# Gated 3x3 convolution pair on one core: four PSUM banks for each sum, the base group 6 units behind, residuals last in a round

## The reference

```python
def qconv_cg(x, w, theta):
    base = cin // CG_GROUPS                       # 64 // 4 = 16 channels
    yp = conv3x3(x[:, :base], w[:, :base])
    yr = conv3x3(x[:, base:], w[:, base:])
    d = jax.nn.sigmoid(CG_ALPHA * (yp - theta[None, :, None, None]))
    return yp + d * yr
...
h = jax.nn.relu(bn(qconv_cg(x, w_a, theta_a), gamma_a, beta_a, mean_a, var_a))
h = bn(qconv_cg(h, w_b, theta_b), gamma_b, beta_b, mean_b, var_b)
return jax.nn.relu(x + h)
```

## Time and profile before

| | |
|---|---|
| median of 3 runs | 456.45 us (455.68 to 456.56) |
| profiled execution, its own time | 456.05 us |
| span from first to last instruction in it | 454.2 us |
| PE busy | 439.9 us (97%) |
| DVE busy | 246.3 us (54%) |
| ACT busy | 209.0 us (46%) |
| matmuls of L383 | 7776, in 1944 units of each of four groups |
| read and written in HBM | 13.14 MB and 12.85 MB |

### The profile page before, as it was taken

One profiled execution on the slowest core, in us unless ns is written; L12 is line 12 of the kernel. 1 busy time (PEld: TensorE's weight loads), 2 busy tenths in 40 slices (PEclk: granted clock), 3 DMA queues, 4 the chain that ended last, 5 costly groups with the idle time before them and its releaser, 6 DMA issues.

```text
span 454.2 us, 16832 instructions
## 1 busy us (share of the span) xinstructions
PE 439.9 (97%) x7801; PEld 436.1 (96%) x7801; DVE 246.3 (54%) x405; ACT 209.0 (46%) x334; POOL 6.8 (1%) x22
## 2 busy tenths in 40 slices
PE   4999999999999999999999999999999999999992
PEld 4999999999999999999999999999999999999992
DVE  6445565365456537544653754575365546435534
ACT  5455645454454445435444533544365344425313
POOL 5000000000000000000000000000000000000000
PEclk9999999999999999999999999999999999999996
DMA  9930000080806280070626044052622121003126
GB/s 164 215 76 2 4 3 1 3 144 2 144 1 113 35 143 4 4 142 3 116 29 144 2 84 63 1 104 43 115 33 47 29 54 21 3 1 74 25 50 141
DMA packets 116388, 27.05 MB, mean 60 GB/s; under 512 B 116192, under 2 KB 116192, under 8 KB 116320
## 3 DMA queue, kind: packets, MB, share of 16 engines
q1 hardware_dynamic: 115408, 25.86, 31.9%
q10 hardware_dynamic: 592, 0.13, 0.1%
q0 software_dynamic: 320, 0.00, 0.0%
HBM read 13.14 MB, written 12.85 MB: 57 GB/s over the span
## 4 chain that ended last, share of the span: by engine, by line
PE 96%; DMA 2%; DVE 1%; ACT 1%; issue 0%; DVEq 0%
PE acc L383 95%; DMA out_dram<-rows_out 1%; DMA w_nat<-in_L_conv_w_a_dram 1%; PE acc L339 1%; DVE rows_out L630 0%; DVE mix L615 0%; DVE mix L613 0%; ACT w_pad L450 0%; ACT rows_out L507 0%; ACT w_hi L443 0%; DVEq L612 0%
## 5 line engine op out<-in xcount | busy, mean ns | idle before, releaser
L383 PE MATMUL acc<-h_hi,w_hi 32*128 32x512 f32 (+1 forms) x1248 | 270.0, 389 | 0.0
L383 PE MATMUL acc<-h_lo,w_hi 32*128 32x512 f32 (+1 forms) x1248 | 268.9, 389 | 0.0
L383 PE MATMUL acc<-x_hi,w_hi 32*128 32x456 f32 x1344 | 267.8, 371 | 0.8 <-ACT w_hi L443 0.8
L383 PE MATMUL acc<-h_hi,w_lo 32*128 32x512 f32 (+1 forms) x1248 | 268.1, 388 | 0.0
L383 PE MATMUL acc<-x_hi,w_lo 32*128 32x456 f32 x1344 | 267.0, 369 | 0.0
L383 PE MATMUL acc<-x_lo,w_hi 32*128 32x456 f32 x1344 | 266.6, 368 | 0.0
L383 PEld LDWEIGHTS acc<-x_hi,w_hi 32*128 32x128 f32 x1344 | 218.9, 187 | 2.3 <-issue 0.9
L383 PEld LDWEIGHTS acc<-x_lo,w_hi 32*128 32x128 f32 x1344 | 218.8, 185 | 0.4
L383 PEld LDWEIGHTS acc<-x_hi,w_lo 32*128 32x128 f32 x1344 | 218.8, 186 | 0.3
L383 PEld LDWEIGHTS acc<-h_hi,w_lo 32*128 32x128 f32 x1248 | 201.1, 183 | 0.2
L383 PEld LDWEIGHTS acc<-h_lo,w_hi 32*128 32x128 f32 x1248 | 200.9, 183 | 0.2
(11 more groups left out here) (52 smaller groups left out, 30.3 us busy)
## 6 DMA issues: line engine op xcount, KB each, us to landing
x<-in_x_dram SPq DMA_DIRECT2D x30, 392.0 KB, 5.2
out_dram<-rows_out SPq DMA_DIRECT2D x30, 392.0 KB, 7.3
out_dram<-rows_out SPq DMA_DIRECT2D x4, 126.0 KB, 2.5
x<-in_x_dram SPq DMA_DIRECT2D x1, 280.0 KB, 4.9
x<-in_x_dram SPq DMA_DIRECT2D x1, 266.0 KB, 5.7
w_nat<-in_L_conv_w_a_dram SPq DMA_DIRECT2D x1, 144.0 KB, 3.1
w_nat<-in_L_conv_w_b_dram SPq DMA_DIRECT2D x1, 144.0 KB, 4.3
x<-in_x_dram ACTq DMA_DIRECT2D x1, 126.0 KB, 3.2
```

Of the source, the lines that this page charges most:

```text
L383: return pe.matmul(sums(bank, blk), w[g * ROWS:(g + 1) * ROWS, tap], moving(blk, part, c, dx, g), start=(u == 0 and (alone or g == FIRST_G ...
```

## The change

yr and yp get four banks each (`b % 4` and `4 + b % 4`). The base group runs 6 units behind group 1, as group 2 does, in place of 20. The transposes of the second weights and of the parameter rows, both in place of steps 13 and 16, are issued at step 5, and the parameter rows go to bank 4. On ACT all four gates of a round come first, each with its x split, then all four finishes. On DVE two x splits, then four products with their sums, then the other two splits, then the four residuals or low parts.

```diff
-YR_BANKS, YP_BANKS = 5, 3
+YR_BANKS, YP_BANKS = 4, 4
-OFFSET = (20, 0, 6, 12)
+OFFSET = (6, 0, 6, 12)
...
-                if step == 13:
+                if step == 5:
                     pe.wait_ge(wlo_ready, 2)
                     weights(1, 6)
-                if step == 16:
+                if step == 5:
                     pe.wait_ge(prmdup_ready, 2)
-                    pe.transpose(psum[:, 5, 0:10], prm_dup[:].rearrange("n c q -> n (c q)"),
+                    pe.transpose(psum[:, 4, 0:10], prm_dup[:].rearrange("n c q -> n (c q)"),
...
-                    if g == 0 and u == 0 and b == 1:
+                    if g == 0 and u == 0 and b == 2:
                         pe.wait_ge(whi_ready, 4)
                         pe.wait_ge(wlo_ready, 4)
...
             for b in range(0, TOTAL, ROUND):
+                for j in range(ROUND):
+                    gate(b + j)
+                    split_ahead(b + j)
+                for j in range(ROUND):
+                    finish(b + j)
...
                 nc.vector.tensor_tensor(mix_rows(b), mix_rows(b), yp_rows(b), ALU.add).then_inc(mixed_ready, 1)
-                if order[b][0] == "b":
-                    residual(b)
...
             for b in range(0, TOTAL, ROUND):
+                for j in range(2):
+                    split_ahead(b + j)
+                for j in range(ROUND):
+                    mix_sums(b + j)
+                for j in range(2, ROUND):
+                    split_ahead(b + j)
+                for j in range(ROUND):
+                    if order[b + j][0] == "b":
+                        residual(b + j)
+                    else:
+                        low_parts(b + j)
```

More of the change, by code:

```diff
@@ L568, in batch_norms @@
                 dve.wait_ge(prmT_ready, 1)
-                nc.vector.tensor_copy(prm[:].rearrange("p k n -> p (k n)"), psum[:, 5, 0:10]
+                nc.vector.tensor_copy(prm[:].rearrange("p k n -> p (k n)"), psum[:, 4, 0:10]
                                       ).then_inc(rvar_ready, 1)
```

## The result

The changed kernel takes 461.33 us in the median of 4 runs (461.18 to 461.62), against 456.45 us (455.68 to 456.56) before. The ratio is 1.0116, with a 95% interval from 1.0101 to 1.0130: slower by 1.2%, where 1.4% was forecast (462.6 us, range 460.2 to 465.3). The profiled execution took 461.62 us with a span of 459.8 us, 5.6 us more than the span before. "The kernel before" and "the changed kernel" are always these two; an experiment's time is given beside the kernel before in the same session, which differed from session to session by up to 0.8 us.

What follows compares the result with a forecast made beforehand. The prediction took PE to bound the 26 rounds, with costs only at the two ends: span 454.2 + 2.3 (start) + 0 (rounds) + 4.2 (end) = 460.7 us, plus 1.85 around it, 462.6 us; range 460.2 to 465.3.

Steps and rivals of the forecast that it cites:

- What bounds the kernel: Whole kernel: a start, 26 rounds bound by PE, and an end of some 14 us; the change moves the ends.
- The start: Before the first product: all groups stand behind the base group's wait for the parameter copy; 2.3 us slower, bounds 1.9 and 3.4.
- 3.2 us behind the fourth group: At the start: PE's clock rises 3.2 us after the fourth group enters at 17.4, so at 20.6 us.
- The rounds: The 26 rounds: four banks still give products enough time; cost 0, bounds -1.4 and +1.5 us.
- The spare 0.35 to 0.4 us at the yr banks: In the rounds: with four banks each product ends 0.35 to 0.4 us before PE needs it, less some 0.1.
- The end: Last round: place 104's residual stands behind four products and sums, so SP's stores start 4.2 us later without shrinking; bounds 3.3, 4.2.
- three pairs of 1.43 us and one of 1.31: Last round on DVE: four products with sums before the first residual, from 440.38 to 445.98 us.
- The sum: Whole kernel: span 454.2 + 2.3 + 0 + 4.2 = 460.7 us, plus 1.85 around it: 462.6 us.
- Rival 1: Rounds: the spare 0.4 us isn't enough; 467.6 us with 0.2 us lost in 25 rounds, 483 in lockstep; chance 0.10.
- the 483 given for the rival's worst case: Rounds: groups in lockstep in all rounds, 0.8 us lost a round, 483 us.
- Rival 2: End: the stores close up behind the last relu, which then sets the end; 457.2 us; chance 0.06.
- Rival 3: Rounds: every one of 26 rounds lost 0.3 us to three yp banks; 7.8 us given back, 454.8; chance 0.02.

Runs made afterwards that it cites:

- e2: The changed kernel with the old order in the last round (each residual right behind its sum, ACT's first relu behind two gates): 457.43 us, ratio 1.0037 to the kernel before.
- e5: The changed kernel with each residual right behind its sum again on DVE, in all rounds: 484.38 us beside 455.86 us of the kernel before.
- e9: The changed kernel with image 14 stored in two parts, its first 23 slots at once: 459.10 us, ratio 1.0074 to the kernel before.
- e4: The kernel before with only its last round in the changed order: 461.67 us, ratio 1.0136 to the kernel before.
- e1: The changed kernel with the parameter rows transposed into bank 3 in place of bank 4: 457.69 us, ratio 1.0044 to the kernel before.
- e8: The kernel before with both transposes at step 5 in place of steps 13 and 16: 454.98 us, ratio 0.9987 to the kernel before.
- e3: The changed kernel with parameter rows in bank 3 and the old order in the last round: 453.85 us, ratio 0.9958 to the kernel before.
- e6: The changed kernel with the base group 12 units behind in place of 6: 475.88 us (2 runs).
- e7: The kernel of e3, with ACT issuing one of the two stores of each piece of the last image: 454.65 us, ratio 0.9973 to the kernel before.
- e10: The changed kernel with parameter rows in bank 3, old order in the last round and image 14 stored in two parts: 452.69 us, ratio 0.9934 to the kernel before.

## Why the prediction was right, point by point

**What bounds the kernel** held: PE's rounds are the same 412 us in both kernels, and all that moved moved at the ends.

**The start**: forecast +2.3 us, measured +2.3 (30.38 against 28.07), by the steps given. The copy ended at 15.23 (15.42 forecast), behind the low and high parts of the weights and image 1's split, just as the chain lists them. The clock reached its upper level at 20.7 (20.6 forecast from "3.2 us behind the fourth group"). That agreement is luck. In kernels with this same start the units came to 0.21 us apart at 19.4 (e2), 20.7 (after), 21.2 (e5) and 21.5 us (e9), which is 2.3 to 4.1 us behind the fourth group's first unit; with the start of before it was 3.2 us in one execution and 1.7 us in the other (e4). The runs give no fixed distance. The first product of kernels with this same start came at 29.67 (e2), 30.38 (after), 30.63 (e5) and 30.72 us (e9), and those with the start of before at 27.33 (e4) and 28.07: means of 30.35 and 27.70, 2.65 us apart, with 0.7 to 1.1 us between executions of one start. What the wait costs beside a kernel without it is more, 3.3 us (e1), since moving the transposes up gains some 0.6 us (e8) once nothing else holds the start.

**The rounds**: forecast 0 between -1.4 and +1.5, measured -0.4 us. It repeats: 412.2 to 412.4 us in the kernels with the old order (before, e4, e8), 411.8 to 411.9 in those with the new one (after, e1, e2, e3). Which part of the change gives the 0.4 us was not tested. The spare 0.35 to 0.4 us at the yr banks was enough, and e5, which takes 0.7 to 1.4 us from it, lost what this reading said, 25.6 us for 26. How many steps PE's sequencer runs ahead of its waits was not tested by itself.

**The end**: the mechanism held, the size was 0.5 us smaller. The term that failed is "three pairs of 1.43 us and one of 1.31": I took the distance from product to next product out of the kernel before, where each operation waits for the result of the one ahead of it. In the changed kernel the product of the next block does not depend on the sum ahead of it, and starts 0.60 us behind it (442.96 to 443.56) in place of 0.71; so does the first residual (446.81 to 447.35). Product to residual took 5.10 us in place of 5.60. From there on 0.77 us to the relu, 0.74 to the store and 8.77 us of stores were as read.

**The sum**: 460.7 us of span forecast, 459.8 measured: 0.5 us of the end, 0.4 us of the rounds. Its own time lies 1.8 us above the span, as added, and 0.3 us above the median of its runs. As a difference to the kernel before, 6.5 us were forecast; the two profiled executions differ by 5.6 us, and the ratio gives 5.3. The range was not added from the bounds as given: it takes 4.4 us for the end where the text had at most 4.2, and -1.0 for the rounds where it had -1.4. With the bounds as given it is 459.9 to 465.2 us, and the measured time lies in either.

**The rivals.** Rival 1 (the spare time isn't enough) did not happen, but e5 and e6 show that it was near: one edit takes the kernel to 484 us. That this is near the 483 given for the rival's worst case is chance, since e5 delays the products by 0.7 to 1.4 us, which the changed kernel does not do. Rival 2 (stores close up) is excluded by SP's 8.76 or 8.77 us in seven profiles (before, after, e1 to e5), and by e7. The Trainium skill's fit ("DMA: Bandwidth & Descriptors", anatomy of a DMA) is given there for one DMA on the GpSimd path; applied to SP's ten stores together, as the prediction did, it gives an estimated 5.7 us from the first store to the last byte's landing. The traces do not agree: from SP's first issue to the end of the span it is 10.9 us in both kernels, 8.8 of them in the issues, at 157 to 173 GB/s (e3, e7) in packets of under 512 B. Rival 3 (the rounds hold more waiting) had 0.4 us to give, not 7.8.

## What to carry to other kernels

When PE is busy 97% of the time, read the two ends: which transfer is the last one, what is queued behind it, and which instruction first lets it start. An order that is good for the steady rounds (products first) can be bad for the last round, where nothing needs the bank any more and the first result is what starts the stores; give the last round its own order, and store early what is complete. And before an engine's in-order stream gets a wait earlier, look at what else of that wait's bank or buffer could be chosen: here another bank for ten parameter rows gave 3.3 us.

## What the runs showed of the hardware

- The time at which TensorE's clock rises from 1.2 to 2.4 GHz varies with no change in the code. It is read here from the distance between units of 456 columns, which falls from 0.38 to 0.21 us; the PEclk column reads 1.00 for the kernel before from 15 to 20 us, where most units are still 0.38 us apart, so at the start it does not tell the level. With one start the units came to 0.21 us apart at 18.1 and 19.7 us (e4, before), with another at 19.4 to 21.5 us (e2, after, e5, e9), with a third at 17.2 and at 14.7 us (e1, e10). The first products of such groups lie 0.7 to 1.1 us apart, as much as some of the edits studied here.
- DVE starts an operation that needs nothing from the one ahead of it 0.60 us behind that one's start, though it lasts 0.68 us; one that waits for that one's result starts 0.71 us behind it (442.96 to 443.56, and 442.25 to 442.96, in the changed kernel).
- With fewer bytes behind the first relu SP's ten stores take 6.71 us, 0.67 us each (e9). On the last stretch one queue gives 157 GB/s where two give 173 (e3, e7).
- A unit of one row group can start ahead of units of others that stand before it in the program. The base group's first unit, of step 20, started at 16.41; step 19's units of the other groups started at 16.70. The Trainium skill ("TensorE: Matmul & The Clock Gate", part 3, on what overlaps) says that matmuls start strictly in program order; these rows do not agree, and neither do those of e4, where the two times are 16.32 and 16.61. From the PE timeline of the kernel before, step 18 and step 19:

```profile
16.32 0.58 PE L383 MATMUL acc<-x_lo,w_hi 32*128 32x456 f32 x1
...
16.70 0.58 PE L383 MATMUL acc<-x_lo,w_hi 32*128 32x456 f32 x1
```
